# Latent attention with its mean squares and denominators computed in 32-column tiles and spread by SBUF transfers, its division on GpSimd, and all fetches of a 64-expert stage issued first

## What is computed

```python
xn = layernorm(x, ln_x_g, ln_x_b)
ln = layernorm(latents, ln_l_g, ln_l_b)
q = (ln @ Wq).reshape(b, m, h, d).transpose(0, 2, 1, 3)
kv = jnp.concatenate([xn @ Wkv, ln @ Wkv], axis=1)
...
qn = rmsnorm(q, qn_g) * scale
kn = rmsnorm(k, kn_g)
sim = jnp.einsum('bhid,bhjd->bhij', qn, kn)
...
attn = jax.nn.softmax(sim.astype(jnp.float32), axis=-1)
out = jnp.einsum('bhij,bhjd->bhid', attn, v)
return out.transpose(0, 2, 1, 3).reshape(b, m, h * d) @ Wout + bout
```

## Time and profile before

| | |
|---|---|
| time, median of 3 runs | 1460.13 us (1458.07 to 1470.2) |
| the profiled execution | 1467.86 us, span 1465.3 us |
| busy in the span | PE 1311.1, DVE 827.5, ACT 700.0, POOL 514.9 us |
| mean granted clock of PE | 0.957 |
| latent attention | from about 449.7 us to 1079.2 us of the span, its rounds from 493.7 us |
| 64-expert stage | its pairs from 325 us to 429 us |

### The profile page before, as it was taken

How to read it: one execution, slowest core, us unless ns; L and a number is a source line. 1 busy time by engine, 2 the same in 40 slices (tenths; PEclk the granted TensorE clock), 3 DMA queues, 4 the chain that set the end, 5 groups by cost and what they waited for, 6 DMA issues and landing times. The chain is left out here.

```text
span 1465.3 us, 19896 instructions
## 1 busy us (share of the span) xinstructions
PE 1311.1 (89%) x7055; PEld 567.5 (39%) x7055; DVE 827.5 (56%) x1364; ACT 700.0 (48%) x1216; POOL 514.9 (35%) x486
## 2 busy tenths in 40 slices
PE   5888789659996899999999999999976998887998
PEld 2213332238972333333333333333334774323443
DVE  3757767272337666656665666566445444623654
ACT  4454444442225666656665666566432444453222
POOL 1012201046621744444554454445414771320000
PEclk9999899779999999999999999999997999898999
DMA  9500310159622000000000000000042124000430
GB/s 260 220 1 12 101 21 1 65 184 383 247 85 87 1 1 1 1 0 2 0 1 0 1 1 1 1 1 1 1 154 62 52 53 130 1 1 1 116 74 15
DMA packets 40109, 85.75 MB, mean 59 GB/s; under 512 B 7582, under 2 KB 23070, under 8 KB 39262
## 3 DMA queue, kind: packets, MB, share of 16 engines
q1 hardware_dynamic: 28044, 70.44, 14.6%
q0 software_dynamic: 4544, 9.32, 2.3%
q10 hardware_dynamic: 7424, 4.72, 1.1%
HBM read 76.56 MB, written 11.04 MB: 60 GB/s over the span
## 5 line engine op out<-in xcount | busy, mean ns | idle before, releaser
L2652 ACT ACTIVATE a_prob<-a_TP 128x512 f32<-128x512 f32 x256 | 138.9, 594 | 123.4 <-PE a_TP L2423 121.7
L2787 DVE TENSOR_REDUCE a_lat<-a_SP 128x2 f32<-128x1024 f32 x128 | 155.7, 1216 | 62.6 <-PE a_SP L2387 62.5
L2915 POOL TENSOR_TENSOR a_acc<-a_prob 128x512 f32<-128x512 f32 x64 | 79.8, 1269 | 232.5 <-ACT a_prob L2652 232.5
L2419 PE MATMUL a_TP<-a_qn,a_kn 64*128 64x512 f32 x512 | 147.5, 641 | 2.6 <-ACT a_prob L2652 2.6
L2435 PE MATMUL a_MS<-a_prob,a_V 128*64 128x512 f32 x512 | 122.6, 599 | 0.2 <-ACT a_prob L2652 0.2
L3470 DVE TENSOR_REDUCE a_nm<-a_A 128x8 bf16<-128x616 f32 x84 | 66.7, 794 | 38.3 <-PE a_A L3153 38.2
L2924 POOL TENSOR_TENSOR a_acc<-a_acc,a_prob 128x512 f32<-128x512 f32 x64 | 80.0, 1274 | 18.4 <-ACT a_prob L2652 18.4
L2419 PEld LDWEIGHTS a_TP<-a_qn,a_kn 64*128 64x128 f32 x512 | 40.4, 184 | 104.3 <-issue 75.3
L2919 POOL TENSOR_TENSOR a_acc<-a_acc,a_prob 77x512 f32<-77x512 f32 x64 | 80.4, 1277 | 0.0
L3684 POOL TENSOR_TENSOR a_on<-a_osb,a_rden 128x512 f32<-128x512 f32 x9 | 11.5, 1280 | 162.6 <-ACT a_osb L3353 162.6
L2423 PE MATMUL a_TP<-a_negm,onesb 64*128 64x512 bf16 (+1 forms) x320 | 64.8, 377 | 0.0
(11 more groups left out here) (553 smaller groups left out, 2856.3 us busy)
## 6 DMA issues: line engine op xcount, KB each, us to landing
ring_w<-in_F_w SPq DMA_DIRECT2D x64, 512.0 KB, 9.1
f_wide<-weight_rows SPq DMA_DIRECT2D x24, 256.0 KB, 5.5
a_maskT<-in_maskT SPq DMA_DIRECT2D x1, 2304.0 KB
a_biasT<-in_biasT SPq DMA_DIRECT2D x1, 2304.0 KB
f_b<-in_F_b SPq DMA_DIRECT2D x1, 2048.0 KB, 9.4
token_rows<-f_xtok ACTq DMA_DIRECT2D x8, 256.0 KB, 8.1
a_biasQ<-in_biasQ SPq DMA_DIRECT2D x3, 616.0 KB, 5.3
ring_w<-expert_rows SPq DMA_DIRECT2D x4, 384.0 KB, 6.2
```

The costliest lines, as they stand in the source:

```text
L2419: nc.tensor.matmul(TP[0:n, h, :], keys(h), qn[half(h), r % 4, :], start=True, stop=False)
L2652: nc.scalar.activation(prob[0:n, 2 * k + h, :], TP[0:n, h, :], ACT.Exp, bias=rowneg[0:n, b:b + 1] if k == 0 else 0.0).then_inc(p_ready, 1)
L2787: nc.vector.tensor_reduce(lat[:, g % 2, 2 * u:2 * u + 2], SP[:, :, :], AX.X, ALU.max, negate=True).then_inc(s_used, 1)
L2915: nc.gpsimd.tensor_tensor(acc[:, h, :], prob[:, 2 + h, :], prob[:, 4 + h, :], ALU.add).then_inc(added, 1)
```

## The change

In `latent_attention`, for pairs 3 to 31 (RAW = 3) the mean squares are computed with a 128 x 32 block (`blk[:, 48:80]`, 16 columns of ones for each head) over halves of 256 tokens (HS): four matmuls (query/key x token half) fill four 32-row strips of one bank with 256 columns. `clip_means`, `rms` then work on 128 x 256, `square_k` writes 128 partitions in one instruction, and SP spreads the result to `rn` with eight SBUF-to-SBUF transfers of 16 source rows, each row read four times. The denominators of rounds 0 to 30 go the same way: four matmuls with a 128 x 32 block of ones, `denominators` on 128 x 256, and four transfers of 32 rows, each read twice, into `rden`. DVE no longer waits for the denominators: `keep_output` copies the raw output out of PSUM and POOL multiplies it in SBUF by `rden` (`divide`), behind `add_chunks`. The order of the loop is changed on PE, ACT and DVE. In `capacity_moe` each pair has its own row buffer, used for the fetched rows and later for the results, and POOL issues all 32 fetches before the first send.

```diff
@@ capacity_moe, gpsimd
-                    for n in range(ROUTED, AHEAD):
+                    for n in range(ROUTED, PAIRS):
                         fetch(n)
                     pool.wait_ge(c.rows_zeroed, 32)
-                    for n in range(AHEAD, PAIRS + AHEAD):
-                        if n < PAIRS:
-                            if n >= FETCH:
-                                pool.wait_ge(rows_turned, n - FETCH + 1)
-                            fetch(n)
-                        if n - AHEAD >= 2:
-                            send(n - AHEAD - 2)
-                    send(PAIRS - 2)
-                    send(PAIRS - 1)
+                    for n in range(PAIRS):
+                        send(n)
@@ latent_attention, sync
+                for r in range(R):
+                    g = r + RAW
+                    if g < R:
+                        sp.wait_ge(ms_rms, g + 1)
+                        for j, normed, spread in ((0, q_normed, q_spread), (1, k_normed, k_spread)):
+                            sp.wait_ge(normed, g)
+                            for n in range(2):
+                                for h in range(2):
+                                    at = 32 * (2 * j + n) + 16 * h
+                                    sp.dma_start(rn[half(h), j, n * HS:(n + 1) * HS],
+                                                 rms_rows[at:at + 16, :].rearrange("i (c t) -> i c t", c=1)
+                                                 .broadcast_to([16, 4, HS])).then_inc(spread, 16)
+                    if r:
+                        sp.wait_ge(den_ready, r)
+                        if r >= 2:
+                            sp.wait_ge(o_normed, r - 1)
+                        for h in range(2):
+                            for n in range(2):
+                                at = 32 * (2 * h + n)
+                                sp.dma_start(rden[half(h), n * HS:(n + 1) * HS],
+                                             den_rows[at:at + 32, :].rearrange("i (c t) -> i c t", c=1)
+                                             .broadcast_to([32, 2, HS])).then_inc(den_spread, 16)
@@ tensor: means(g), sums(r)
+                    if g >= RAW:
+                        for j in range(2):
+                            for n in range(2):
+                                at = 32 * (2 * j + n)
+                                mm = nc.tensor.matmul(MS[at:at + 32, 0, 0:HS], blk[:, HD - 16:HD + 16],
+                                                      mine[:, j, n * HS:(n + 1) * HS], start=True, stop=True)
+                        mm.then_inc(ms_ready, 1)
+                        return
...
-                    if r + 1 < R:
-                        pe.wait_ge(negm_ready, r + 2)
                     for h in range(2):
+                        if r == R - 1:
...
+                        for n in range(2):
+                            at = 32 * (2 * h + n)
+                            mm = nc.tensor.matmul(DEN[at:at + 32, 0:HS], ones64[:, 0:32],
+                                                  acc[:, h, n * HS:(n + 1) * HS], start=True, stop=True)
@@ tensor: the loop over r, steps s
-                        if s == 0 and r:
-                            values(r - 1, 3)
-                            values(r - 1, 4)
-                            sums(r - 1)
-                            if r < 2 * B:
-                                later_values(r)
-                        if s == 1 and r + 3 < R:
+                        if s == (0 if r else 1) and r + 3 < R:
...
                             project(r + 3)
-                        if s == 2:
+                        if s == 1 and r:
+                            values(r - 1, 3)
+                        if s == (1 if r else 2):
...
                             if r + 3 < R:
+                                means(r + 3)
+                        if s == 2 and r:
+                            values(r - 1, 4)
+                            if r + 3 < R:
+                                pe.wait_ge(ms_clipped, r + 4)
+                            sums(r - 1)
+                        if s == 3:
+                            if p == 0 and b:
+                                output(b - 1, O, range(NP))
+                            else:
+                                for k in range(3):
+                                    values(r, k)
+                        if s == 4:
+                            if r + 1 < R:
                                 if r:
                                     pe.wait_ge(den_log, r)
...
                                 turn(r + 1)
                             if has_values(r):
                                 make_values(r)
+                            if 0 < r < 2 * B:
+                                later_values(r)
+                            if p == 0 and b:
+                                pe.wait_ge(x_updated, b)
+                                for k in range(3):
+                                    values(r, k)
@@ scalar: the loop over r
+                    if r and has_values(r - 1):
+                        copy_values(r - 1)
+                    if 1 < r <= 2 * B:
+                        keep_later(r - 1)
                     for k in range(NK):
                         exponentials(r, k)
...
-                        if k == 1 and r + 3 < R:
+                        if k == (0 if r else 1) and r + 3 < R:
                             square_q(r + 3)
                             square_k(r + 3)
-                        if k == 3 and r + 3 < R:
+                        if k == (1 if r else 3) and r + 3 < R:
                             rms(r + 3)
+                        if k == 2 and r:
+                            denominators(r - 1)
@@ vector: the loop over r
-                    if r:
-                        normalise(r - 1)
                     if r + 1 < R:
                         reduce(r + 1, 2)
+                    if 0 < r < R - 3:
+                        clip_means(r + 3)
+                    if r + 1 < R:
                         reduce(r + 1, 3)
...
+                    if r:
+                        keep_output(r - 1)
                     if r + 1 < R:
                         reduce(r + 1, 4)
                         combine(r + 1)
                     if r + 3 < R:
                         norm_q(r + 3)
+                        norm_k(r + 3)
+                    if p == 0 and b:
+                        dve.wait_ge(prep, 7)
+                        update(b - 1, O)
+                    if r + 2 < R:
+                        reduce(r + 2, 0)
                     if r + 1 < R:
                         shift(r + 1)
-                    if r + 2 < R:
-                        reduce(r + 2, 0)
-                    if r + 3 < R:
-                        norm_k(r + 3)
                     add_last(r)
@@ gpsimd
+                def divide(r):
+                    pool.wait_ge(o_kept, r + 1)
+                    pool.wait_ge(den_spread, 64 * (r + 1))
+                    nc.gpsimd.tensor_tensor(on[:, r % NP, :], on[:, r % NP, :], rden[:, :],
+                                            ALU.mult).then_inc(o_normed, 1)
...
                 for r in range(R):
                     add_chunks(r)
+                    if r:
+                        divide(r - 1)
```

More of the change, by code:

```diff
@@ L1602, in capacity_moe @@
             src, dest = sb("src", [P, PAIRS], U32), sb("dest", [P, PAIRS], U32)
-            xs = sb("xs", [P, FETCH, D])
+            rows = [sb(f"row{n}", [P, D]) for n in range(ROUTED)]
             b_loaded, lists_ready = sem("b_loaded"), sem("lists_ready")
-            rows_in = [sem(f"rows_in{i}") for i in range(FETCH)]
+            rows_in = [sem(f"rows_in{n}") for n in range(PAIRS)]
             def fetch(n):
                 nc.gpsimd.indirect_dma_start(
-                    out=xs[:, n % FETCH, :], out_offset=None, in_=c.xrows[:, :],
-                    in_offset=bass.IndirectOffsetOnAxis(ap=src[:, n:n + 1], axis=0)).then_inc(rows_in[n % FETCH], 16)
+                    out=rows[n][:, :], out_offset=None, in_=c.xrows[:, :],
+                    in_offset=bass.IndirectOffsetOnAxis(ap=src[:, n:n + 1], axis=0)).then_inc(rows_in[n], 16)
             with ExitStack() as own:
@@ L1931, in capacity_moe @@
             hb, hg = sb("hb", [P, 2, 512]), sb("hg", [P, 2, 512])
-            ys = sb("ys", [P, SEND, D])
+            rows += [sb(f"row{n}", [P, D]) for n in range(ROUTED, PAIRS)]
             HP = ctx.enter_context(nc.psum_tensor(name + "_HP", [P, 2, 512], F32))
@@ L1938, in capacity_moe @@
                 sem(n) for n in ("rows_turned", "xs_ready", "h_ready", "b_added", "gelued", "y_ready", "y_kept"))
-            rows_out = [sem(f"rows_out{i}") for i in range(SEND)]
+            rows_out = sem("rows_out")
             fetched = [sem(f"fetched{i}") for i in range(2 * B)]
@@ L1965, in _ @@
                         ring.load(sp, n)
-                    for i in range(SEND):
-                        sp.wait_ge(rows_out[i], 16 * (PAIRS // SEND))
```

(18 more changed lines are left out.)

92 lines of the change are left out of this document (45 added, 47 removed).

## The result

| | before | after |
|---|---|---|
| median of 20 runs each | 1465.76 us | 1456.97 us |
| ratio after / before, 95% interval | | 0.9947 [0.9932, 0.9962] |
| the profiled execution, its span | 1467.86 / 1465.3 us | 1462.04 / 1460.3 us |
| attention, first round to the next stage (span) | 586.8 us | 580.7 us |

The change saves 0.53%, 7.8 us (5.6 to 10.0), where the forecast was 18.2. The ratio leaves out two executions of each kernel that took some 3% longer than the rest, so it isn't quite the quotient of the medians. The time lies at the upper edge of the range given, and the kernel before is itself 5.6 us slower here than the 1460.1 that the forecast started from. "Faster", which the prediction set at 14.6 us or more and gave 0.63, did not come; its "same", at 0.25, did. The mechanism was the one forecast; more than half of its gain is missing, and the traces say where.

What follows compares the result with a forecast made beforehand. PE's stream was taken to bound the attention stage. Full rounds -19.3, first round +3.8, rounds 29 to 31 -2.7, batches and 64-expert stage 0: -18.2 us, from the 1460.1 median to 1442 us, range 1430 to 1458.

Steps and rivals of the forecast that it cites:

- same: Whole kernel: a change within 1% of 1460 us (14.6 us), given a chance of 0.25.
- The 32-column blocks: Sums and mean squares on PE: 0.57 us each instead of 0.96 and 1.02, bounds 0.50 and 1.00.
- The output waits for the division: First round of three batches: the last product waits 1.3 us for the division, replacing a 1.43 us clip wait; net 0.
- Rounds 0 and 1: Start of attention: one wait of 3.0 to 3.5 us for the first transfers, +3.8 us in all.
- The 64-expert stage: All fetches issued before the sends: worth 0, bounds -1 and +2 us.
- a single chunk is four records of 512 columns, the form of a sums block with its exit, 0.96: Value chunks on PE, now in two steps: two cost 1.92 us against 1.77 as a pair.
- The first rival: Small PE blocks cost 0.75 us instead of 0.57 because draining and loading tiles isn't covered; 1452 us, chance 0.2.
- the transfers cost nothing: Mean-square transfers in each round: landed by 13.1 to 13.6 us, 1.1 to 1.6 us before key normalisation must start.
- The second rival: SP's issue or the landing of the spread transfers becomes the bound, slower than before; about 1489 us, chance 0.12.
- The 1 us that it adds for the clock: Start of attention: after the wait PE runs at the lower clock level, 1 us more, bounds 0 and 4.
- Rounds 29 to 31: Last attention rounds: a value chunk and the sums fill PE's waits for exponentials, 0.9 us a round, -2.7 us.
- None of these engines sets the round, so they count as nothing: Attention rounds: changed work on ACT, DVE and POOL priced at 0, though POOL's grows by 1.27 us a round.

Runs made afterwards that it cites:

- shift_first: Changed kernel, but in rounds 8 to 28 DVE computes the shift before normalising the keys; 0.9948 [0.9924, 0.9972] of the kernel before.
- latent_only: Changed attention stage with the 64-expert stage of the kernel before; 0.9944 [0.9923, 0.9965] of the kernel before.
- all_four: Changed kernel, pair 3 in old form, division after last additions in rounds 29-31, shift before key normalisation, denominators' transfers and division earlier at batch starts; 0.9861 of before.
- second job: The changed kernel unaltered, run again beside variants of it; 0.9957 [0.9936, 0.9978] of the kernel before, median 1456.59 us.
- late_divide: Changed kernel, but in rounds 29 to 31 POOL divides only after DVE's last additions; 0.9939 of the kernel before, 0.9945 when run again.

## Why the prediction was off

**What held.** PE's stream sets the round, and no transfer, no DVE and no POOL work took its place: 16.5 us in 13 of the 17 plain rounds from 9 to 27. The 32-column blocks cost 0.57 us. The output waits for the division, 1.21, 1.18 and 1.20 us (1.3 forecast). Rounds 0 and 1 wait for the first transfers, 3.9 us together (3.0 to 3.5 forecast). The 64-expert stage stays as it is.

The forecast for the attention rounds was -18.2 us, the traces say -9.1 without the dip. The 9.1 us between them:

**A block's neighbour (1.8 us in the 18 rounds without a batch's start or later values).** The step "a single chunk is four records of 512 columns, the form of a sums block with its exit, 0.96" is mis-sized: the earlier trace rows gave a pair of chunks only. Two single chunks cost 2 x 1.01, and the round is 16.51 or 16.52 instead of 16.42. What stands behind the chunk sets this: ahead of the block of 64-column tiles a chunk costs 0.91, ahead of that of 32-column tiles 1.01. The two blocks differ in the width of their tiles and also in the number and length of their matmuls, and no run separates these. The first rival looked for this on the wrong side: it put the drain into the small block, which is 0.57, and not into the chunk before it. Its total, 1452 and -8 us, lies close to the result by luck: its mechanism carries only 1.8 of the 9.1 us. The Trainium skill ("TensorEngine Tiling (Array Packing)", Key Properties) has a change of tiling mode drain TensorE; the 0.10 us between the two pairs of rows agrees with it without showing it alone, and is small. Rounds 2 to 7, where the later values moved too, saved 0.74 each instead of 0.69: 0.3 us back.

**Transfers that are covered in most rounds only (1.8 us in four plain rounds).** The step that had SP issue a transfer every 0.465 us and all of them landed at 13.1 to 13.6, so that "the transfers cost nothing", failed in its size: 0.63 an issue, `norm_k` at 14.75, and the margin was nearly gone. The earlier trace rows are loads, and a row of four doesn't show the one slow issue (up to 1.49 us) that makes a round 0.3 to 0.5 us longer. `norm_k` is released by a transfer in all 29 rounds, which the prediction had named as a sign that it would be wrong. The second rival's mechanism was there, below the point from which it decides.

**First rounds of a batch (1.3 us).** The waits for clip and division changed places as forecast (1.43 for 1.2). But two of the three rounds took 25.93 and 25.26 instead of 25.05, because they start with a late shift; in `shift_first` all three take 25.04 to 25.06.

**Rounds 0 and 1 (1.0 us).** The waits are 2.08 and 1.82 us, 3.9 together where 3.0 to 3.5 were forecast: from SP's release in round 0 to the last landing it is 6.9 us, not 5.3 to 5.8. The rest of this term came out near by luck. The 1 us that it adds for the clock isn't in this execution (granted clock 1.00 in round 1); in `latent_only`, with a dip there, the two rounds take 40.03 us. In its place 0.7 us come from a dip that both kernels have at the stage's start: in after it lies wholly in round 0 (492.68 to 496.09, the round starts at 492.58), in before only its last 2.0 us do (until 495.68, the round starts at 493.70).

**Rounds 29 to 31 and the end (3.5 us).** "None of these engines sets the round, so they count as nothing" is the step that failed. POOL's division got no price on DVE, and at the end of the stage nothing stands behind DVE's last additions to cover them. Moving the division behind them gives 1.9 us back. Round 29 also pays for a late shift, 0.38 to 0.72 us by the execution, and 0.31 us for one of DVE's reduces. What is left of the 3.5, under 1 us, is not traced to one step. In `all_four`, which has neither, the stretch takes 56.9 us, 2.4 less than before: close to the 2.7 that the moved blocks were to bring.

By the ratios the gain is 7.8 us (5.6 to 10.0), and in the second job 6.3 (3.2 to 9.4). Both hold the 6.1 of the two traces as they stand. The 9.1 without the dip lies inside both as well; the three executions with the stage of after each lose 1 to 3 us to a dip in one place or another behind the stage's start, and one of the two with the stage of before does.

## What to carry to other kernels

Cover is a margin to be measured in the worst round, not in the usual one: a transfer that is hidden by 0.5 us costs time in every round in which one of its eight issues is slow, and the slow ones come at much the same places in every execution. Work given to an idle engine is free only where it shares nothing with the busy ones; look for two-input SBUF instructions that run beside it, first at the end of a stage, where nothing covers them. When one profile says 5 us and the ratio says 1, compare the granted clock in both before believing the 5, and take a second profile of the same kernel.

## What was unexpected of the hardware

**An SBUF instruction with two inputs on DVE does not run beside one of POOL; it waits for its end.** Alone, DVE's two additions take 1.28 us (at 658.24 in after; 0.68 for one). At the end of after they start at 1056.57, POOL's division ends at 1057.64 + 1.27 = 1058.91, and they end at 1056.57 + 3.49 = 1060.06, 1.15 us later. The first of them lost its turn twice there: it started during POOL's last addition, which ends at 1057.69, and did not get on before the division behind that had ended too. In `late_divide` POOL's last addition ends at 1054.92 and DVE's pair at 1056.07, again 1.15 later. `combine`, 8 columns wide, shows it best. First before, then after, with POOL's instructions at that time (in pairs of 1.27 us each):

```profile
674.78 2.52 POOL L2919 TENSOR_TENSOR a_acc<-a_acc,a_prob 77x512 f32<-77x512 f32 x2
...
675.29 0.83 DVE L2798 TENSOR_TENSOR a_nm<-a_lat,a_con 128x8 bf16<-128x8 f32 x1
```

```profile
686.90 2.50 POOL L2980 TENSOR_TENSOR a_acc<-a_prob 128x512 f32<-128x512 f32 x2 [5.86 <-PE a_MS L2472]
...
689.15 0.30 DVE L2855 TENSOR_TENSOR a_nm<-a_lat,a_con 128x8 bf16<-128x8 f32 x1
```

Both end with POOL's current instruction (about 676.04, the first of the pair, and 689.40, the second), within 0.1 us: 838 ns on average in rounds 9 to 28 before, 306 after, for the same work. It holds throughout: of the 32 `combine` in after, 31 start beside an instruction of POOL, and each of these ends 0.05 us behind the end of it; of the 64 additions 44 do, and 43 of these end 0.55 us behind it, the other being the one that lost twice. The Trainium skill ("SBUF — State Buffer", SBUF: two separate sides) says just this: DVE with two SBUF inputs and a GpSimd instruction that reads SBUF contend for a port pair that one of them holds for a whole instruction. The rows agree to 0.1 us. By it the division's price on the last additions could have been estimated beforehand as one more POOL instruction, 1.27 us; 2.48 - 1.27 = 1.21 was measured.

**The issue of an SBUF-to-SBUF transfer** costs SP 0.59 us in the median for the mean squares, 0.54 to 1.49, against 0.43 to 0.47 of the loads in the earlier trace rows, and 0.60 with plain source rows.
